# Two attention layers of a graph network: weighted sums run beside the score gathers, in four parts

## The reference

```
q = x@Wq+bq; k = x@Wk+bk; v = x@Wv+bv; e = edge_weight * We
alpha = sum_over_32(q[dst] * (k[src] + e)) / sqrt(32)         # per edge and head
p     = exp(alpha - segment_max(alpha, dst)[dst])
out   = segment_sum((v[src] + e) * p, dst) / segment_sum(p, dst) + x@Ws + bs
```

## Time and profile before

| | us |
|---|---|
| median of three runs | 11805.8 |
| profiled execution, device time | 11822.46 |
| its span | 11820.6 |
| GpSimd busy | 8006.9 (68%) |
| TensorE busy | 8681.5 (73%) |
| VectorE busy | 7482.5 (63%) |
| ScalarE busy | 6380.5 (54%) |

### The profile page before, as it was taken

The page is one execution under the profiler, slowest core; times in us unless marked ns, Lnnn a source line. Parts: engine busy times, 40 slices in busy tenths (PEclk is TensorE's granted clock), DMA queues, the critical chain, the costliest instruction groups (busy, mean ns, idle before and its releaser), DMA issues. The chain is left out here.

```text
span 11820.6 us, 295566 instructions
## 1 busy us (share of the span) xinstructions
PE 8681.5 (73%) x56071; PEld 6458.3 (55%) x56072; DVE 7482.5 (63%) x21356; ACT 6380.5 (54%) x16838; POOL 8006.9 (68%) x8175
## 2 busy tenths in 40 slices
PE   5887788788778868886887888688855555555555
PEld 2776677555455546654554555465544445444444
DVE  5877777555566766766666666667643348633368
ACT  4544454444455555555555555555555546455555
POOL 2777777677577757766775777577557766477755
PEclk7998899799889989998998999899976669765678
DMA  2111111222244434434443444344245544455544
GB/s 56 31 31 33 35 31 30 61 56 56 58 117 111 110 96 111 112 89 117 110 111 96 111 110 111 97 111 111 77 135 157 157 134 138 122 157 157 157 115 116
DMA packets 1310031, 1161.81 MB, mean 98 GB/s; under 512 B 238842, under 2 KB 1105822, under 8 KB 1308784
## 3 DMA queue, kind: packets, MB, share of 16 engines
q0 software_dynamic: 272544, 566.00, 19.1%
q1 hardware_dynamic: 1036816, 589.72, 17.6%
HBM read 1005.76 MB, written 149.12 MB: 98 GB/s over the span
## 5 line engine op out<-in xcount | busy, mean ns | idle before, releaser
L978 POOL DMA_INDIRECT rings<-rows_key,idx x4536 | 4364.7, 962 | 1914.6 <-issue 1327.4
L1162 DVE TENSOR_TENSOR bigDE<-bigDE,part 128x128 f32 (+1 forms) x6656 | 1890.4, 284 | 1420.1 <-PE part L1073 435.4
L1073 PE MATMUL part<-rings 128*128 128x128 f32 (+1 forms) x11920 | 1712.9, 290 | 645.7 <-ACT rings L1014 245.1
L1086 PE MATMUL wide<-bigDE,bigC 128*128 128x384 bf16 x10800 | 1964.1, 339 | 239.6 <-DVE bigC L1144 217.8
L599 POOL DMA_INDIRECT bigDE<-rows_key_value,idx x1664 | 1573.0, 945 | 677.2 <-issue 677.2
L1073 PEld LDWEIGHTS part<-rings 128*128 128x128 f32 (+1 forms) x11920 | 1558.7, 190 | 823.7 <-issue 751.1
L1005 ACT ACTIVATE rings<-iota,relK 128x128 f32<-128x128 f32 x5960 | 1900.4, 389 | 5.1 <-issue 1.5
L978 POOL DMA_INDIRECT rings<-rows_hidden,idx x1424 | 1386.7, 974 | 595.5 <-issue 409.9
L997 ACT COPY idx<-srcK 128x4 int32 (+1 forms) x1490 | 283.6, 191 | 2531.7 <-PE part L1073 2342.9
L1086 PEld LDWEIGHTS wide<-bigDE,bigC 128*128 128x128 bf16 x10800 | 1074.3, 101 | 986.3 <-issue 397.3
L647 PE MATMUL part<-bigB,bigDE 128*128 x3328 | 784.4, 408 | 964.9 <-ACT bigDE L629 961.7
(11 more groups left out here) (309 smaller groups left out, 10558.8 us busy)
## 6 DMA issues: line engine op xcount, KB each, us to landing
rings<-in_attr SPq DMA_DIRECT2D x3780, 64.0 KB
walk_value<-bigDE SPq DMA_DIRECT2D x416, 256.0 KB, 3.0
rings<-walk_value SPq DMA_DIRECT2D x416, 256.0 KB
rings<-rows_key,idx POOLq DMA_INDIRECT x4536
bigDE<-rows_key_value,idx POOLq DMA_INDIRECT x1664
bigF<-in_attr SPq DMA_DIRECT2D x380, 64.0 KB
rings<-rows_hidden,idx POOLq DMA_INDIRECT x1424
rows_key<-rings SPq DMA_DIRECT2D x60, 320.0 KB, 2.6
```

The lines of the kernel that those rows point to most:

```text
L978: e.indirect_dma_start(to[:, r, 0:width], None, table, bass.IndirectOffsetOnAxis(ap=idx[:, r:r + 1], axis=0)).then_inc(gate.sem, 16)
L1073: last = e.matmul(part[0:width, bank(n), r, :], msg[:, r, 0:width], sel[:, r, :], start=True, stop=True)
L1086: last = e.matmul(wide[:, r, 0:3 * width], hot[:, r * P:r * P + P], room.pieces(s, 1).rearrange("p a j f -> p (a j f)"), start=s == 0, sto ...
L1162: e.tensor_tensor(into, into, got, ALU.add).then_inc(c.added.sem, 1)
```

## The change

`_look` and `_softmax` become one stage, `_converse`, and the 208 groups are cut into four parts of 40, 48, 56 and 64 groups (`SPANS`).

- Part 0: scores alone, as before.
- The first 8 groups of parts 1 to 3 (`FRESH`): scores as before, and after each group one of eight steps of the softmax of the part before (`soft_part`). The maximum is a running one: a run of equal destinations that goes over a part's edge carries the maximum in from the part before, and the sums made so far for that one node are scaled by exp(old maximum - new maximum).
- The other groups of parts 1 to 3 (40 + 48 + 56 = 144): scores of group q beside the weighted sums of group p = q - `SPANS[k]` of the part before. SyncE reads the values of p (`load`) ahead of writing those of q (`store`); VectorE, and no longer GpSimd, multiplies the values with the weights, one group ahead (`blend`); TensorE multiplies in two halves (`scatter`); VectorE adds into one set of sums (`add`), each sum after the one before it.
- After part 3: its softmax alone, with the skip term, and then `_attend` for its 64 groups only.

In the second layer `bigA` serves as working space. So the first layer writes it to DRAM (`held`) at the start of its stage, and the second layer reads it back (3200 KB) on SyncE's queue, ahead of the value loads of `_attend`. The sums are cleared at the start of `_converse`.

The core of the diff:

```diff
+SPANS = (40, 48, 56, 64)
+STARTS = (0, 40, 88, 144)
+FRESH = 8
@@ _converse, SyncE
+            def load(i, g):
+                q = i * RING + g
+                e.wait_ge(c.blended.sem, c.blended.at(q - 1))
+                e.dma_start(value[:, g % 2, :, :], spill[bass.ds(q, 1), ...]).then_inc(c.attrs[g].sem, 16)
+                with _loop(e, begin + FRESH // RING, end) as i:
+                    for g in range(RING):
+                        load(i - SPANS[k] // RING, g)
+                        store(i, g)
@@ _converse, ScalarE
+                        if not (final and g == RING - 1):
+                            extend(k - 1, q + 1, (g + 1) % RING)
+                        look(i, g)
+                        if g % 2 == 0:
+                            draw(q + 2, (g + 2) % RING)
@@ _converse, TensorE
+            def scatter(i, g):
...
+                _hold(e, c.blended, q + 1, c.tick_pe)
+                for half in range(2):
+                    e.wait_ge(c.added.sem, c.added.at(q * GROUP + (2 * half + 2 - GROUP)))
+                    for r in (2 * half, 2 * half + 1):
+                        done = e.matmul(halves[:, half, r % 2, 0:cell], marks[:, g, r, :], msg[:, g % 2, r, :],
+                                        start=True, stop=True)
+                        turned_to(i, g)
+                        ask(i, g)
+                        scatter(i - SPANS[k] // RING, g)
@@ _converse, VectorE
+                        tell(q, b)
+                        multiply(i, g)
...
+                        add(p, where[b * GROUP], 0)
+                        reduce(q, b)
+                        add(p, where[b * GROUP + 1], 1)
+                        if b == 0:
+                            mark(p + 3, (g + 3) % RING)
...
+                            blend(i + ((g + 1) // RING - SPANS[k] // RING), (g + 1) % RING)
+                        add(p, where[b * GROUP + 2], 2)
+                        finish(q, b)
+                        add(p, where[b * GROUP + 3], 3)
@@ build
-            _look(c, both, c.Bwide, score, spill, weights=queries("2") if conv == 0 else ())
-            _softmax(c, score, told, dram, odd, agg, x, C, column["L3_gnn_bs" + tag])
-            _attend(c, agg, odd, score, told, spill, weights=skips("2") if conv == 0 else ())
+            told = _converse(c, both, c.Bwide, agg, odd, score, spill, dram, x, C, column["L3_gnn_bs" + tag], spare,
+                             weights=queries("2") + [(held, A)] if conv == 0 else ())
+            _attend(c, agg, odd, score, told, spill, weights=skips("2") if conv == 0 else [(A, held)])
```

More of the change, by code:

```diff
@@ L34 @@
 SEQ_ROWS = 32
-SEQ = PAIRS * P // SEQ_ROWS
-SEQ_PAIRS = PAIRS // SEQ_ROWS
+SPANS = (40, 48, 56, 64)
+STARTS = (0, 40, 88, 144)
+FRESH = 8
+assert sum(SPANS) == GROUPS and all(b == a + FRESH for a, b in zip(SPANS, SPANS[1:]))
 FAR = -1.0e30
@@ L582, in _, with bounds @@
+            def bounds(k):
+                src = dram.seq[STARTS[k] * GROUP * P:STARTS[k] * GROUP * P + SEQ_ROWS * seq(k)].rearrange(
+                    "(c x) -> c x", x=seq(k))
+                wide = bass.AP(src.tensor, src.offset, [[seq(k), SEQ_ROWS], [1, seq(k) + 2]])
+                for h in range(HEADS):
+                    e.dma_start(flags(k)[h * SEQ_ROWS:(h + 1) * SEQ_ROWS, :], wide).then_inc(c.moved.sem, 16)
             _load(c, e, weights)
-            with _loop(e, 0, ROUNDS) as i:
+            bounds(0)
@@ L621, in _, with skipped @@
+            def skipped(chunks):
+                for n in chunks:
+                    e.wait_ge(c.applied.sem, c.applied.at(n + 1))
+                    e.activation(skip[:, n * CHUNK:(n + 1) * CHUNK], skips[:, n % 4, 0:CHUNK], ACT.Identity,
+                                 bias=offset).then_inc(c.chunked.sem, 1)
+            for q in range(2):
+                index(0, q)
             select(0, 0)
-            with _loop(e, 0, ROUNDS) as i:
+            with _loop(e, *rounds(0)) as i:
                 for g in range(RING):
[L624 to L630, removed]
+                    look(i, g)
@@ L632, in _ @@
+            soft_part(last, 0)
+            skipped(range(CHUNKS // 2))
+            skipped(range(CHUNKS // 2, CHUNKS))
+            soft_part(last, 5)
+            soft_part(last, 7)
         @block.tensor
         def _(e):
-            with _loop(e, 0, ROUNDS) as i:
-                for g in range(RING):
[L636 to L650, removed]
@@ L652, in _ @@
+            soft_part(last, 0)
+            e.wait_ge(c.joined.sem, c.joined.at(GROUPS))
+            skipped(range(CHUNKS // 2))
+            soft_part(last, 1)
+            soft_part(last, 2)
+            skipped(range(CHUNKS // 2, CHUNKS))
+            for n in range(3, FRESH):
+                soft_part(last, n)
         @block.vector
         def _(e):
-            with _loop(e, 0, ROUNDS) as i:
-                for g in range(RING):
[L656 to L671, removed]
@@ L672, in _look, with tell @@
-    for g in (c.product, c.turned, c.told, c.joined, c.message, c.scored, c.keyed):
-        g.passed(GROUPS)
+            def tell(q, b):
+                weight = c.wK[:, bass.ds(q * GROUP, GROUP)].unsqueeze(2).to_broadcast([P, GROUP, HEADS])
+                e.wait_ge(c.product.sem, c.product.at(q + 1))
+                e.tensor_tensor(edge[:, b, :].rearrange("p (r h) -> p r h", h=HEADS),
+                                part[:, b, :, D:D + HEADS], weight, ALU.mult).then_inc(c.keyed.sem, 1)
@@ L674, in _look @@
+            for n in range(FRESH):
+                soft_part(last, n)
+    for gate in (c.product, c.turned, c.joined, c.message, c.scored):
+        gate.passed(GROUPS)
+    c.keyed.passed(2 * GROUPS)
     c.select.passed(GROUPS + 1)
@@ L680, in _look @@
         g.passed(16 * ROUNDS)
+    early = STARTS[last]
+    for g in c.attrs:
+        g.passed(16 * early // RING)
+    c.blended.passed(early)
+    for gate in (c.scattered, c.expanded):
+        gate.passed(2 * early)
+    c.added.passed(early * GROUP)
+    for gate in (c.drawn, c.marked):
+        gate.passed(early // 2 + 1)
+    c.close.passed((early // 2 + 1) * GROUP)
+    c.lined.passed(step(last, 58))
+    c.moved.passed(16 * HEADS * len(SPANS))
+    c.applied.passed(CHUNKS)
+    c.chunked.passed(CHUNKS)
+    c.cleared.passed(2)
+    return told(last)
 def _attend(c, agg, odd, score, told, spill, weights=()):
+    first = STARTS[-1]
+    groups = SPANS[-1]
+    rounds = groups // RING
     nc = c.nc
@@ L698, in _ @@
             _load(c, e, weights)
[L699 removed]
+            with _loop(e, 0, rounds) as i:
                 for g in range(RING):
```

563 lines of the change are left out of this document (385 added, 178 removed).

## The result

| | us | range of the runs |
|---|---|---|
| before, four runs | 11809.59 | 11804.28 to 11814.54 |
| after, four runs | 11964.67 | 11959.66 to 11979.77 |
| forecast | 11295 | 11220 to 11510 |

The ratio after to before is 1.0134, with a 95% interval of 1.0116 to 1.0151: 155 us slower, where 511 us of gain were forecast. The prediction was wrong, in sign too.

The account below looks back on a forecast made before the run. GpSimd's gather issue was taken as the bound. Per layer 1048.6 + 10 + 20 + 48 + 110 = 1236.6 us against 1497.1; two layers less 10 for `bigA` save 511, so 11295 us, range 11220 to 11510.

Parts of the forecast that it names:

- What bounds it: In the score stage, GpSimd's gather issue is the limit: four gathers of 1.25 us, 5.0 us a group.
- The sum of each engine's work: In the joint loop, per group: VectorE 4.3 us, ScalarE 4.2, TensorE 3.97, GpSimd 5.0, so GpSimd is longest.
- The loop between the engines: In the joint loop, the chain from the last add through TensorE, ScalarE and VectorE: 4.4 us a period, under 5.0.
- The slack: In the score stage, GpSimd can stand 9.8 us of delay in the other engines before it stalls.
- Fresh groups: Three stretches of 8 groups holding softmax steps: 20 us of stalls a layer, ends 0 and 106.
- Last softmax, last sums, `bigA`: After part 3: 48 us for softmax, 110 for weighted sums; 10 for reading `bigA` back, second layer only.
- Rival 1: Joint loop: TensorE's clock stays low or loops are longer, 5.9 us a group, 228 us more, 11523; chance 16%.
- Rival 2: Everything hides: no slip in the joint loop, no fresh stalls, 60 us less, 11235; chance 10%.
- Rival 3: Joint loop: VectorE's operations with two SBUF inputs hold GpSimd, 297 us, 11592; chance 5%.
- Rival 4: Joint loop: transfers are the bound at 156 GB/s, 6.7 us a group, 475 us more, 11770; chance 4%.
- Rival 5: Joint group runs in series, 8.8 us, 1070 us more, 12365; change slower from 6.9 us a group; chance 4%.
- slower issues: Joint loop: gather issues of 0.967 us at most beside busy VectorE, against 0.945; 10 us a layer taken.

Follow-up runs that it names:

- ScalarE's order: Changed kernel with `extend` (two copies of weights) moved from the head of ScalarE's step to its end: 11377.31 us, ratio to before 0.9625.
- both orders: Changed kernel with `extend` at the end of ScalarE's step and TensorE's next transposes ahead of the scatter: 11345.55 us, ratio to before 0.9602.

## Why the prediction was wrong, point by point

**What bounds it (held for before only).** The gather issue was the bound, and became it again, at 5.25 us a group, as soon as ScalarE's order was mended. In the changed kernel it was not: GpSimd was idle 359.5 us for the index copy in one layer and as much in the other, 719 together, near the 670 us by which the forecast missed.

**The sum of each engine's work (right).** VectorE was put at 4.3 us a group, ScalarE at 4.2, TensorE at 3.97. In the stretch of 320 us with 44 groups it measures 149.29 / 44 = 3.4, 171.68 / 44 = 3.9 and 191.29 / 44 = 4.3. Busy time counts what overlaps once; the durations add up to 3.93 us for VectorE and 4.17 for ScalarE, as summed. TensorE's is higher, at a lower clock than was taken. All are under 5.0, and none of them explains 7.2.

**The loop between the engines (the step that failed).** The prediction summed one loop, "the last add of group p-1 frees half of the scatter of p (0.57), behind which stand the transposes of q+1 (0.97), ScalarE's copy (0.58) and the products of q+1 (1.86)", and gave it two periods. It took ScalarE's copy to run when the transposes are done. ScalarE's list says otherwise: ahead of that copy stand the 0/1 matrix, the index copy and, at the head, `extend`, which waits for the scatter of the period before. That puts 2.62 us of ScalarE in series with the copy, the products and the scatter, all within one period. The prediction had every duration for this: 0.40 + 0.193 + 2.0 + 0.577 on ScalarE, 1.86 and 1.14 on TensorE, together 6.2 us before any semaphore or change of clock, already far over 5.0. Measured: 7.17 by the timeline, 7.2 by the gathers. The 1.0 us between them is the scatter (2.29 to the copy of weights behind it, not 1.14) and 0.38 from ScalarE's copy to the products, less 0.56 that the products were faster. The error is 7.22 x 144 = 1039.7 us against 735.8 for the joint groups, 304 us a layer, 608 of the 670 us by which the forecast missed. That moving `extend` gives 587 us, 566 of them in the joint groups, shows it.

**The slack (right, and no help).** "A constant offset within the 9.8 us of slack" holds of an offset. A loop longer than 5.0 us eats it at 2 us a group; the longest wait of GpSimd for an index copy is 7.7 us.

**Fresh groups (the size was off).** 163.5 us a layer (48.7 + 56.4 + 58.4) against 140: 43 us of stall where 20 were taken and 106 was the upper end. It is 33 us with ScalarE's order mended and 18 with both orders, so over half of it was the order on these two engines and not the softmax's own work.

**Last softmax, last sums, `bigA` (right).** 45.0 against 48, with the one slow copy that was allowed for: it started at 10056.46 us beside GpSimd's clearing of 5.76 us.

```profile
L950 DVE COPY bigDE<-bigF x8: 356/361/2983, 10056.5 to 11718.8; 128x256 f32<-128x256 f32 x8
```

111.5 against 110. `bigA` was asked for at 11753.44 us and the first read of values was issued at 11760.14, 6.7 us against 10. GpSimd's first product on these values starts 13.8 us after the rescaling of the sums, against 7.6 in the first layer, which puts it at 6.2.

**The rivals.** Rival 1 (low clock, longer loops; 5.9 us a group, 11523) named the right family with a wrong mechanism: its price was every matmul at the lower level, with GpSimd or TensorE the bound. The clock itself was worth 111 us by the experiment for the rise from 0.70 to 0.85; what the rest of the way is worth in this loop no run shows. Rival 2 (all hides) is wrong. Rival 3 is a real mechanism, once the gathers bound: 48 us of the 297 priced. Rival 4 (a ceiling of 156 GB/s) is refuted by 200 GB/s in the joint loop of both orders. Rival 5, the series case, held in its threshold, slower from 6.9 us a group, and in its side; 7.2 was reached. But it had VectorE waiting in series with all the others (8.8 us), while in the trace VectorE's work lies beside the loop between ScalarE and TensorE. It had 4%; a loop added up in the order of ScalarE's list would have made it the forecast.

**The forecast of another kernel.** With the failed step mended the sum is good: 11345.55 us measured with both orders, 11295 forecast. Of the 50 us between them 44 lie in the joint groups, 756 and 759 us in the two layers against 736 each, and there the held gather issues are the cause: without them the joint groups take 733 us a layer. The forecast had 10 us a layer for slower issues, too little. The rest agrees within a few us (the fresh groups 138.4 against 140, the last softmax 44.3 against 48).

## What to carry to other kernels

When work of an earlier group is put into a loop beside a later group's, write down for each engine the first instruction of its step that waits, and everything behind it in the list, and add up the chain until it comes back to itself within one period; the sum of an engine's work says nothing of this. Put what waits for another engine's last result at the end of a step, behind everything that others wait for: two copies of 0.2 us at the head of a step cost 587 us here. An engine that waits for no one before the change is the thing to check after it, since its first wait for a neighbour names the loop.

## What the runs showed of the hardware

A gather issue on GpSimd that starts while VectorE runs an operation of 0.69 us with two SBUF inputs is held, here until about the operation's end. In the kernel with both orders the timeline of a stretch reads (start, duration, engine, line)

```profile
9196.35 0.69 DVE L924 TENSOR_TENSOR bigC<-rings,bigF 128x512 f32<-128x512 f32 x1
...
9196.57 1.28 POOL L692 DMA_INDIRECT bigDE<-rows_key_value,idx  x1 [0.30 <-issue]
...
9200.66 0.95 POOL L692 DMA_INDIRECT bigDE<-rows_key_value,idx  x1 [0.30 <-issue]
...
9201.04 0.68 DVE L924 TENSOR_TENSOR bigC<-rings,bigF 128x512 f32<-128x512 f32 x1
```

The first started 0.22 us into the operation and took 0.34 us longer than the usual 0.94; the second was under way when the operation began, and took its usual time. It is so throughout 9160 to 9390 us: of 177 issues 31 took over 970 ns, and each of them started inside one of the two operations (L924, L913), the longer the more of it was left; the 33 issues that were under way when one began took 956 ns at most, and the 95 that met neither 957. With one-input sums in place of these operations the longest issue in the window was 956 ns, against 1354 ns. The median (946, 947) shows none of it. The prediction took the median, 944 ns in the edge layers, as speaking against a hold; the mean there is 965, so those rows could not rule one out. The Trainium skill, "SBUF — State Buffer", section "Who interferes with whom", says that a VectorE instruction with two SBUF inputs contends with a GpSimd instruction that reads SBUF; the runs agree, if an indirect issue counts as one that reads.

More matrix work shortened the changed kernel, in which TensorE's results were waited for: with the transposes made three times, the granted clock in the joint loop rose from 0.70 to 0.85, and the run was 111 us shorter. With the gathers as the bound the same work raised the clock from 0.91 to 0.99 and gave nothing (11385 us against 11377).
